# Flamingo cross-attention block: pairs of weighted sums moved together in TensorE's order

## The reference, cut to what matters

```python
qh = (q @ Wq.T).reshape(Bq, Nq, Hh, Dh).transpose(0, 2, 1, 3)
kh = (k @ Wk.T).reshape(Bq, Lk, Hh, Dh).transpose(0, 2, 1, 3)
vh = (v @ Wv.T).reshape(Bq, Lk, Hh, Dh).transpose(0, 2, 1, 3)
attn = jnp.einsum('bhnc,bhlc->bhnl', qh * scale, kh)
attn = jax.nn.softmax(attn, axis=2)
attn = attn / jnp.sum(attn, axis=-1, keepdims=True)
out = jnp.einsum('bhnl,bhlc->bhnc', attn, vh)
...
x = x + jnp.tanh(g_xattn[0]) * _L0_xattn_ref(_layernorm(x, axis=-1), ctx_1024, ctx_1024, L0_xattn_Wq, L0_xattn_Wk, L0_xattn_Wv, L0_xattn_Wo)
x = x + jnp.tanh(g_ffn[0]) * _L0_ffn_ref(_layernorm(x, axis=-1), L0_ffn_router_w, L0_ffn_w1, L0_ffn_w2)
```

## Time and profile before

| what | value |
|---|---|
| runs | 1795.82, 1798.08, 1798.51 us; median 1798.08 |
| the profiled execution's own time | 1794.36 us |
| its span, first to last instruction | 1792.6 us |
| mean granted TensorE clock | 0.996 of full speed |
| TensorE matmuls (PE) busy | 1703.8 us, 95% |
| VectorE (DVE) busy | 1417.2 us, 79% |
| ScalarE (ACT) busy | 1283.0 us, 72% |
| GpSimd (POOL) busy | 538.2 us, 30% |
| exps on ScalarE, L934 | 1664, busy 1128.9 us |
| negmax on VectorE, L1114 | 832, busy 1001.9 us |
| score matmuls, L732 | 1664, busy 532.9 us |
| weighted sums, L745 | 3328, busy 443.7 us |

### The profile page before, as it was taken

How to read it: one execution, slowest core, us unless ns; L and a number is a source line. 1 busy time by engine, 2 the same in 40 slices (tenths; PEclk the granted TensorE clock), 3 DMA queues, 4 the chain that set the end, 5 groups by cost and what they waited for, 6 DMA issues and landing times.

```text
span 1792.6 us, 31795 instructions
## 1 busy us (share of the span) xinstructions
PE 1703.8 (95%) x10074; PEld 918.3 (51%) x10074; DVE 1417.2 (79%) x2293; ACT 1283.0 (72%) x3653; POOL 538.2 (30%) x821
## 2 busy tenths in 40 slices
PE   8999999999999999999999999889999999999997
PEld 5233334333333433333333342225899999999997
DVE  7998999999999999999999999997344444444442
ACT  5999999999999999999999999996111111111111
POOL 3331252352343225235223422213122222222222
PEclk9999999999999999999999999999999999999999
DMA  8546226414712721551371163419222222222221
GB/s 231 139 121 183 66 70 158 129 40 123 187 47 62 198 72 52 158 154 40 102 187 51 51 172 75 154 52 326 67 37 35 36 37 35 38 35 35 36 37 27
DMA packets 128247, 172.90 MB, mean 96 GB/s; under 512 B 14496, under 2 KB 105760, under 8 KB 128128
## 3 DMA queue, kind: packets, MB, share of 16 engines
q1 hardware_dynamic: 113152, 150.51, 30.8%
q0 software_dynamic: 14144, 20.44, 6.6%
q10 hardware_dynamic: 832, 0.53, 0.1%
HBM read 117.96 MB, written 53.47 MB: 96 GB/s over the span
## 4 chain that ended last, share of the span: by engine, by line
ACT 40%; PE 30%; DVE 20%; issue 7%; DMA 2%; POOL 1%; SPq 0%; POOLq 0%; DVEq 0%; ACTq 0%
ACT w_all L934 37%; DVE negmax L1114 14%; PE scores L1507 14%; PE scores L1520 13%; ACT w_all L879 1%; ACT parts L870 1%; DVE resid L1009 1%; DMA out<-row_t,gate_token 1%; PE spare L1497 1%; DVE rz L1100 1%; PE scores L732 1%; PE spare L593 1%; DVE x L1025 1%; DVE stats L1133 1%; DVE stats L1143 0%
## 5 line engine op out<-in xcount | busy, mean ns | idle before, releaser
L934 ACT ACTIVATE w_all<-scores,negmax 128x512 f32<-128x512 f32 (+1 forms) x1664 | 1128.9, 778 | 19.9 <-DVE negmax L1114 15.4
L1114 DVE TENSOR_REDUCE negmax<-scores 128x2 f32<-128x1024 f32 (+1 forms) x832 | 1001.9, 1215 | 53.8 <-PE scores L732 47.4
L732 PE MATMUL scores<-q_stack,w_all 128*128 128x512 bf16 (+1 forms) x1664 | 532.9, 385 | 42.1 <-ACT w_all L934 34.3
L934 ACT ACTIVATION_READ_ACCUMULATOR w_all<-scores,negmax 128x1 f32 (+1 forms) x1664 | 495.2, 298 | 0.0
L745 PE MATMUL acc<-w_all,vz 128*32 128x512 f32 (+1 forms) x3328 | 443.7, 605 | 0.0
L732 PEld LDWEIGHTS scores<-q_stack,w_all 128*128 128x128 bf16 (+1 forms) x1664 | 136.8, 99 | 575.2 <-ACT w_all L934 514.6
L1553 ACT ACTIVATE projections<-scores 128x512 f32<-128x512 f32 x142 | 84.8, 597 | 445.8 <-PE scores L1507 440.2
L1337 POOL TENSOR_TENSOR vz<-w_all,rz 128x68 f32<-128x68 f32 (+1 forms) x416 | 124.5, 299 | 776.3 <-DVE rz L1100 751.0
L1507 PEld LDWEIGHTS scores<-row_t,q_stack 128*128 128x128 f32 x2272 | 264.4, 192 | 7.0 <-issue 2.0
L1507 PE MATMUL scores<-row_t,q_stack 128*128 128x128 f32 x2272 | 265.6, 275 | 1.9 <-DVE row_t L1580 1.9
L1520 PE MATMUL scores<-room,projections 128*128 128x256 f32 x1136 | 256.8, 379 | 0.0
(11 more groups left out here) (215 smaller groups left out, 1048.9 us busy)
## 6 DMA issues: line engine op xcount, KB each, us to landing
w_all<-k_parts SPq DMA_DIRECT2D x248, 200.1 KB, 3.5
w_all<-in_w SPq DMA_DIRECT2D x16, 1024.0 KB, 10.0
q_stack<-q_parts SPq DMA_DIRECT2D x248, 64.0 KB, 3.3
k_parts<-parts SPq DMA_DIRECT2D x42, 300.0 KB, 2.9
w_all<-in_ctx_t SPq DMA_DIRECT2D x7, 1601.0 KB, 7.1
parts<-routed SPq DMA_DIRECT2D x71, 129.0 KB
q_parts<-parts SPq DMA_DIRECT2D x14, 384.0 KB, 3.9
routed<-pad_row SPq DMA_DIRECT2D x8, 645.0 KB
```

What stands on the lines that cost most here:

```text
L732: mm = pe.matmul(scores[0:r, 2 * (u % SLOTS) + j % 2, :], k_stacks[g][:, j, lt * P:lt * P + r], q_stack[:, g, j, :], start=True, stop=True)
L934: act.activation(probs[0:r, s % RING, j, :], scores[0:r, 2 * (u % SLOTS) + j % 2, :], ACT.Exp, bias=negmax[0:r, u % 4, j % 2:j % 2 + 1], a ...
L1114: dve.tensor_reduce(negmax[0:r, u % 4, :], scores[0:r, 2 * (u % SLOTS):2 * (u % SLOTS) + 2, :], AX.X, ALU.max, negate=True).then_inc(negma ...
```

## The change

A new function `weighed` plans, for a batch, which weighted sums each step does and where. Ahead of a step in which a piece begins (`begins_behind`), the step does no weighted sum. The step itself then does two, s-4 and s-3, back to back between its first and its second pair. It applies where s-3 isn't the first tile of a group, as the special order did before. Elsewhere nothing moves.

```diff
     def begins_behind(self, s):
 
         begun = any(halves == (0,) for _, halves in self.halves(s))
-        return begun and self.fill(s - 1) is not None and (s - LAG) % LT > 0
+        return begun and self.fill(s - 1) is not None
+
+    def weighed(self):
+
+        plan, following = [], 0
+        for s in range(STEPS):
+            due = s - LAG
+            behind, at_end = range(0), range(0)
+            if following <= due:
+                if self.begins_behind(s) and due % LT > 0:
+                    behind, following = range(following, due + 1), due + 1
+                elif not (s + 1 < STEPS and self.begins_behind(s + 1) and (due + 1) % LT > 0):
+                    at_end, following = range(following, due + 1), due + 1
+            plan.append((behind, at_end))
+        return plan
...
         def run(it):
-            for s in range(STEPS):
-                late = s >= LAG and it.cur and it.begins_behind(s)
+            for s, (behind, at_end) in enumerate(it.weighed()):
                 if it.cur:
                     unit_scores(it.b, s, 0)
-                if late:
-                    weigh(it.b, s - LAG)
+                for step in behind:
+                    weigh(it.b, step)
+                if behind and not it.fill(s):
                     unit_scores(it.b, s, 1)
                 for f, halves in it.halves(s):
                     fill(it, *f, halves)
                 if it.tail and s == LOGITS - 1:
                     first_logits(it)
-                if it.cur and not late:
+                if not (behind and not it.fill(s)):
                     unit_scores(it.b, s, 1)
-                    if s >= LAG:
-                        weigh(it.b, s - LAG)
+                for step in at_end:
+                    weigh(it.b, step)
                 if s < LAG and it.tail:
                     weigh(it.b - 1, STEPS + s - LAG)
```

## The result

The changed kernel takes 1810.06 us in the median of five runs, the kernel before 1796.50 us in the five runs beside them: ratio 1.0076, 95% interval 1.0057 to 1.0094. It is 13.6 us slower; 10.4 were forecast.

A forecast was written before the change was run, and what follows sets the result against it. ScalarE was taken to pace the attention, with VectorE and TensorE close behind. Six middle batches at 1.45 us (8.7), the first 0.8 and the last 0.9 sum to 10.4 us slower: median 1808.5 us, range 1799 to 1819.

The forecast's parts named there:

- The way a pair becomes late: With (s, p) as pair p (0 or 1) of step s: (s, 1) starts 3.00 us behind the second exp of (s-2, 1).
- The saving: On TensorE, two weighted sums together save 0.22 us a place, 22 us in 99 places; TensorE's time, not the kernel's.
- Steps 6 and 7: Pair (6, 1) comes 0.59 us late; 0.18 is absorbed and 0.41 us reaches ScalarE's exp of (7, 1).
- Steps 10 to 12: Pair (10, 1) comes 0.48 us late and VectorE's chain carries all 0.48 to ScalarE's exp at step 12.
- Step 39: Pair (39, 1) comes 0.55 us late; a margin of 0.29 leaves 0.26 us.
- The other eleven places: Remaining places of a middle batch: 0.3 us together, an estimate, bounded by nothing and 2.9.
- The first batch: Without out_proj and statistics of the output, so neither large term, but with 13 places: 0.8 us.
- The last: The last batch has the places of steps 6 and 8: 0.41 and about as much again, 0.9 us.
- The signs I named: Profile after: ScalarE's idle time before exps some 30 us, its negmax wait about 26, a middle batch's period 152.75 us.
- Rival 1: TensorE paces and its saving shows at steps 34 to 46: faster, about 1790 us; chance 0.10.
- Rival 2: The delays are absorbed, with 0.5 of cover at step 7 instead of 0.18: no change, 1800 us; chance 0.16.
- Rival 3: Lateness lands at most places, 0.26 us at each of 99: 26 us slower, 1824 us; chance 0.14.

The follow-up runs named there:

- ahead: The changed kernel with both sums back to back at the end of step s-1, before the first pair of step s: 1805.62 us against 1793.00 before, ratio 1.0071.
- three_places: The changed kernel with two sums together only at steps 6, 10 and 39 of the six middle batches: 1802.98 us against 1795.29 before, ratio 1.0049.
- quiet_places: The changed kernel with two sums together only at steps 14, 25, 36, 41 and 43 of the middle batches: 1795.93 us against 1795.29 before, ratio 1.0009.
- before_stats_early: The kernel before with four statistics of x moved from steps 7, 11, 12 and 13 to steps 0 to 3: 1808.93 us against 1793.00, ratio 1.0088.
- dose_three: The kernel before with the second pair's first score matmul made three times at steps 6, 10 and 39 of middle batches: 1802.61 us against 1795.29, ratio 1.0042.
- dose_quiet: The kernel before with the second pair's first score matmul made three times at steps 14, 25, 36, 41 and 43 of middle batches: 1796.74 us, ratio 1.0010.

## Why the prediction was right, and by how much each term was off

The medians differ by 13.6 us where 10.4 were forecast. That the forecast of 1808.5 lies only 1.6 us from the measured median is in part luck, since the kernel before measured 1.6 us less in five runs than in the three from which the forecast started.

**The way a pair becomes late** held to a few hundredths. I put the second pair at 3.00 us behind the second exp of (s-2, 1). At step 6 it is 3.00 (501.79 to 504.79). Steps 10 and 39 of the changed kernel, timeline:

```profile
513.43 0.70 ACT L948 ACTIVATE w_all<-scores,negmax 128x512 f32<-128x512 f32 x1
...
516.46 0.61 PE L746 MATMUL scores<-q_stack,w_all 128*128 128x512 bf16 x2
...
517.10 1.22 DVE L1128 TENSOR_REDUCE negmax<-scores 128x2 f32<-128x1024 f32 x1 [0.53 <-PE scores L746]
...
518.36 0.69 ACT L948 ACTIVATE w_all<-scores,negmax 128x512 f32<-128x512 f32 x1
...
523.98 0.68 ACT L948 ACTIVATE w_all<-scores,negmax 65x512 f32<-65x512 f32 x1 [0.88 <-DVE negmax L1128]
...
599.56 0.78 ACT L948 ACTIVATE w_all<-scores,negmax 128x512 f32<-128x512 f32 x1
600.49 0.39 PE L746 MATMUL scores<-q_stack,w_all 128*128 128x512 bf16 x1 [0.94 <-ACT w_all L948]
...
602.66 0.60 PE L746 MATMUL scores<-q_stack,w_all 128*128 128x512 bf16 x2
...
603.30 1.23 DVE L1128 TENSOR_REDUCE negmax<-scores 128x2 f32<-128x1024 f32 x1 [1.01 <-PE scores L746]
...
604.56 0.69 ACT L948 ACTIVATE w_all<-scores,negmax 128x512 f32<-128x512 f32 x1 [0.19 <-DVE negmax L1128]
```

There it is 3.03 (513.43 to 516.46) and 3.10 (599.56 to 602.66).

**The saving** of 0.22 us a place is there: at 98 of the 99 places the two sums take 1.92 or 1.93 us, as in the earlier trace rows, and at the last they fall into a stretch at half clock. It bought nothing, as said, and the ahead kernel shows that even without the wait for banks it buys nothing. The rule of the Trainium skill that a change of tiling mode drains TensorE ("TensorEngine Tiling (Array Packing)", Key Properties) agrees with this saving, though no run here shows that a drain is its cause; a gain in time, as the rule alone would have it, did not come.

**Steps 6 and 7**: 0.41 forecast, 0.43 measured, at the exp named.

**Steps 10 to 12**: 0.48 forecast, 0.51 measured, but not where I put it. I had it travel down VectorE's chain to the exp at step 12. More than half, 0.28, is already at the exp of (10, 1) at 518.36, where I had overlooked that ScalarE had little to spare: in the kernel before that negmax ended at 513.05 and its exp began at 513.30; 0.14 and 0.09 follow at step 11, and the idle time of 0.88 before 523.98 is hardly more than the 0.84 of the earlier trace rows. The size was right, since a delay of the chain's head reaches ScalarE once, early or late.

**Step 39**: 0.26 forecast, 0.37 measured; the pair was 0.64 late and not 0.55, since (39, 0) got its bank later (600.49, 0.93 behind the exp, in place of 0.82).

**The other eleven places** were the mis-sized term: 0.3 forecast, 0.65 measured (0.18 at step 23, 0.32 at 33, 0.15 at 49). In six batches the 0.35 more make 2.1 us, most of what the sum lacks. It lay inside the bounds, nothing to 2.9.

**The first batch** takes 1.04 us more to the next batch's first exp, where 0.8 was forecast; kernels that leave this batch alone scatter over 0.6 there (149.25 to 149.86). **The last** is 0.56 us shorter between its first and last exp where 0.9 was to come. The kernel before has a stretch at half TensorE's clock at steps 0 and 1 there, which costs 1.1 us; beside three_places and quiet_places, which have the last batch of the kernel before and no such stretch, the changed kernel is 0.6 longer. In all the last exp of the run starts 12.5 us later (1241.4 against 1228.9). Without the stretches at half clock, 1.5 in the changed kernel and 1.1 in the one before, it would be about 12.

**The rest of the span**, from the last exp to the end, was to stay as it was. It took 563.7 us before and 566.9 after in the two profiled executions. Other kernels of this study, with the same experts' part, show 560.9 (before_stats_early) to 565.2 us (three_places). The granted clock goes with this. In this part of the span, up to the last matmul, it is half for 3.4 us in the kernel before and for 13.7 in the changed one, whose window from 1260 to 1400 us reads:

```profile
1260.00:1400.00 140.00, 134.97 (x923) 127.45 (x922) 61.89 (x97) 20.30 (x34) 34.13 (x23) 0.95 0.28 66
```

The same window of the kernel before, which has its only such stretch just ahead, at 1255.8, reads a clock of 1.00 in place of 0.95. Half of the 10.2 us of difference, 5.1, is an upper estimate of what it costs, since TensorE also waits in these stretches. In the twelve profiled executions this part takes from 560.9 to 566.9 us; less half of the time at half clock it is 559.2 to 562.1. So the clock is the likely cause of the 3.2 us. Whether the change has a part in it wasn't tested.

The signs I named were partly wrong in size. ScalarE's idle time was to rise to 30 us and its wait for negmax to 26, and they rose to 27.1 and 21.1. The profile's idle times do not hold all of the lateness: the exp at 518.36 is 0.28 us late, and its row lists none. The period was to be 152.75 us and is 153.10. Rival 1 is refuted by quiet_places, which saves 30 times 0.22 us of TensorE and gains nothing. Rival 2's cover at step 7 was not there. Rival 3, a loss at every place, is refuted by quiet_places too.

## What to carry to other kernels

Where one engine feeds another through a short ring of banks, ask of a reordering when each handover becomes ready, not how much work it saves: two pieces of 0.9 to 1.1 us between neighbouring handovers made one of them half a microsecond late, and that came through wherever the consumer had no queue. Gaps of the feeding engine that come from waiting for banks can't be filled by moving work behind the wait. A place that shows no loss may be hidden by the one ahead of it, so price a change with single places switched on, and read the period of a repeating stretch. Within a trace it repeated to 0.02 us apart from the stretches at half clock, and two kernels with the same middle batches differed by 0.10 (151.11 and 151.01), where medians of runs left 2. Where one instruction is long or one batch late, read the granted clock over it first.

## What the runs showed of the hardware that was not expected

**Single stretches of 3.4 us at half clock in the middle of the attention.** One of six middle batches of the changed kernel is 1.5 us longer than the others. The two sums of step 14, timeline, in the batch before it and in this one:

```profile
680.35 1.92 PE L759 MATMUL acc<-w_all,vz 128*32 128x512 f32 x16
...
833.44 3.57 PE L759 MATMUL acc<-w_all,vz 128*32 128x512 f32 x16
```

And the window over the second, with the columns of the earlier trace rows:

```profile
833.60:836.90 3.30, 3.30 (x16) 0.44 (x8) 2.59 (x4) 3.19 (x11) 2.06 (x4) 0.50 0.26 93
```

Both stand 39.72 us behind the first exp of their batch and are the same 16 matmuls. TensorE doesn't pause: it is busy throughout, at a granted clock of 0.50, the lower of its two levels (1.2 in place of 2.4 GHz), from 833.6 to 837.0. Ahead of it TensorE made four single score matmuls, each after a wait of 0.28 to 0.40 us for an exp. The other middle batches have the same order there and no such stretch.

Every long middle batch of the other traces has such a stretch too. In dose_three two of six middle batches are longer (152.66 and 152.59 us from first to last exp in place of 151.06), in dose_quiet two and in ahead one, each with a stretch at 0.50 while ScalarE is at steps 15 and 16. The middle batches of the kernel before have none and take 149.91 us within 0.01, but its last batch has one at its start, in which a single sum takes 1.77 us (at 1088.35) where the same sum in quiet_places takes 1.06 (at 1088.07). Which batch is hit differs from kernel to kernel; why wasn't tested.

The long wait of before_stats_early shows a longer stretch. While VectorE waits its 18.2 us, TensorE is without a matmul from 32.7 to 51.2 us, and the granted clock is half from 35.0 to 55.5. The first scores after the wait, two matmuls, take 1.28 us, where two took 0.59 before it.
